# An f32r router with row transposes, weight columns by VectorE, outputs copied by ScalarE and added by transfer, statistics among the first taps

## The reference

```
x = x + attn(layernorm(x))      # Q,K,V = x@wq.T, x@wk.T, x@wv.T ; energy = K.T@V ; Q@energy*sqrt(3/64)@wo.T
x = x + ffn(layernorm(x))
# ffn, with h the normed rows (T x 256):
scores = sigmoid(h @ Wr)                      # 8 experts
_, idx = top_k(scores + router_bias, 2)
w  = scores[idx] / (sum(scores[idx]) + 1e-9)  # scattered into cw (T x 8)
hid = silu(h @ Wg[e]) * (h @ Wu[e])           # 4 MLP experts, 128 wide
routed = sum_e cw[:, e] * (hid @ Wd[e])
routed += cw[:, 4]*h + cw[:, 6]*h + cw[:, 7]*relu(h)
ffn = routed + depthwise causal conv of h over 4 rows + conv_b
```

## Time and profile before

| what | value |
|---|---|
| median of 3 runs | 886.65 us (884.33 to 886.78) |
| the profiled execution, its own time | 888.19 us |
| its span | 886.4 us |
| PE busy | 852.9 us, 96% |
| DVE busy | 751.2 us, 85% |
| ACT busy | 643.2 us, 73% |
| POOL busy | 409.6 us, 46% |
| mean granted clock of TensorE | 0.988 |

### The profile page before, as it was taken

One profiled execution on the slowest core, in us unless ns is written; L12 is line 12 of the kernel. 1 busy time (PEld: TensorE's weight loads), 2 busy tenths in 40 slices (PEclk: granted clock), 3 DMA queues, 4 the chain that ended last, 5 costly groups with the idle time before them and its releaser, 6 DMA issues.

```text
span 886.4 us, 16852 instructions
## 1 busy us (share of the span) xinstructions
PE 852.9 (96%) x5437; PEld 757.1 (85%) x5437; DVE 751.2 (85%) x2093; ACT 643.2 (73%) x1366; POOL 409.6 (46%) x585
## 2 busy tenths in 40 slices
PE   5878999999999999999999999999999999899997
PEld 4667888999889988889899998889988998788886
DVE  4668889988899988999899998999889988678884
ACT  4585867787777777787678777777867875666653
POOL 3214635554455454455355544545535544433332
PEclk9899999999999999999999999999999999999999
DMA  9112354433354442434443344554424344324434
GB/s 286 60 43 54 119 144 138 112 110 100 116 143 143 143 120 67 126 125 138 143 121 104 100 132 120 143 144 126 111 75 131 109 121 119 96 54 118 118 94 119
DMA packets 79447, 103.86 MB, mean 117 GB/s; under 512 B 6528, under 2 KB 58880, under 8 KB 79360
## 3 DMA queue, kind: packets, MB, share of 16 engines
q1 hardware_dynamic: 74752, 86.02, 30.6%
q0 software_dynamic: 4608, 16.78, 10.0%
HBM read 68.96 MB, written 17.04 MB: 97 GB/s over the span
## 4 chain that ended last, share of the span: by engine, by line
PE 77%; DVE 12%; ACT 4%; issue 3%; POOL 2%; DMA 1%; POOLq 0%; DVEq 0%; ACTq 0%
PE ps_gu L410 11%; PE ps_gu L412 10%; PE ps_gu L411 10%; PE ps_sh L541 6%; PE ps_y L410 6%; PE ps_y L411 6%; PE ps_y L412 6%; PE ps_y L460 3%; PE ps_sh L531 3%; PE ps_sh L484 2%; ACT x L842 2%; PE ps_sh L588 1%; PE ps_sh L589 1%; PE ps_gram L618 1%; PE ps_gu L564 1%
## 5 line engine op out<-in xcount | busy, mean ns | idle before, releaser
L1391 POOL TENSOR_TENSOR gate<-gate,cwb 128x512 f32<-128x512 f32 x128 | 168.0, 1313 | 291.4 <-ACT gate L765 265.6
L410 PE MATMUL ps_gu<-x2T_hi,wgu_hi 128*128 128x512 f32 x512 | 211.3, 413 | 1.2 <-DVE hid L1055 1.2
L412 PE MATMUL ps_gu<-x2T_hi,wgu_lo 128*128 128x512 f32 x512 | 202.2, 395 | 0.0
L411 PE MATMUL ps_gu<-x2T_lo,wgu_hi 128*128 128x512 f32 x512 | 201.7, 394 | 0.0
L410 PE MATMUL ps_y<-wd_hi,hid_hi 128*128 128x256 f32 x512 | 153.1, 299 | 2.2 <-DVE hid_lo L1062 2.2
L1073 DVE SCALAR_TENSOR_TENSOR conv<-x2T,conv_w,conv 128x512 f32<-128x512 f32 x192 | 150.6, 822 | 0.0
L411 PE MATMUL ps_y<-wd_lo,hid_hi 128*128 128x256 f32 x512 | 145.4, 284 | 0.0
L412 PE MATMUL ps_y<-wd_hi,hid_lo 128*128 128x256 f32 x512 | 145.0, 283 | 0.0
L1062 DVE TENSOR_TENSOR hid_lo<-hid,hid_hi 128x512 fp32r<-128x512 f32 x101 | 86.2, 853 | 46.2 <-ACT hid_hi L758 46.2
L412 PEld LDWEIGHTS ps_gu<-x2T_hi,wgu_lo 128*128 128x128 f32 x512 | 96.6, 189 | 22.2
L410 PEld LDWEIGHTS ps_gu<-x2T_hi,wgu_hi 128*128 128x128 f32 x512 | 97.2, 190 | 18.4 <-issue 2.3
(11 more groups left out here) (126 smaller groups left out, 1877.5 us busy)
## 6 DMA issues: line engine op xcount, KB each, us to landing
cwb<-cw_rows SPq DMA_DIRECT2D x128, 256.0 KB, 4.0
xa<-in_x SPq DMA_DIRECT2D x32, 512.0 KB, 7.8
acc<-in_x SPq DMA_DIRECT2D x32, 512.0 KB, 6.9
acc<-x POOLq DMA_DIRECT2D x32, 512.0 KB, 4.6
out<-acc SPq DMA_DIRECT2D x64, 256.0 KB, 2.6
cwb<-in_wg SPq DMA_DIRECT2D x4, 128.0 KB, 3.9
cwb<-in_wu SPq DMA_DIRECT2D x4, 128.0 KB, 3.7
cwb<-in_wd SPq DMA_DIRECT2D x1, 512.0 KB, 4.5
```

The costliest lines, as they stand in the source:

```text
L410: nc.tensor.matmul(dst, a_hi, b_hi, start=start, stop=False, skip_group_check=True)
L411: nc.tensor.matmul(dst, a_hi, b_lo, start=False, stop=False, skip_group_check=True)
L412: return nc.tensor.matmul(dst, a_lo, b_hi, start=False, stop=stop, skip_group_check=True)
L1391: g.tensor_tensor(gate[:, e % 2], gate[:, e % 2], cwb[:, q, e], ALU.mult).then_inc(gatew_ready, 1)
```

## The change

The router weights are split in halves side by side (`wr2`, 16 columns). `router` now multiplies with them as the stationary side, 512 rows at a time, in f32r: two products with `x2T_hi`, two with `x2T_lo`. The result is 16 x 512. ScalarE copies it (`logitsT`), TensorE turns it back in four transposes (`logits_rows`), and VectorE sums the halves (`logits_sum`). ScalarE makes the size from the sum, after `hid_hi` (1), where `mag` and `dip` now stand too. `cw` is transposed by VectorE in blocks of 32 x 32, so SP stores it in four pieces. In steps 8 to 33 ScalarE copies `ps_y` to `y_rows` and a transfer of GpSimd's queue adds it to `acc`; in the others VectorE adds as before. The aggregation of the first norm's statistics stands behind `x2T_lo` (0). In step 7 the taps are made ahead, in the head, and the statistics after them. In step 33 the residual and the second norm's statistics stand ahead of the routing.

```diff
@@
+    def by_transfer(self):
+        return self.on("Y") and self.on("C") and not self.drain()
@@ SP
                 sp.wait_ge(cwT_ready, st.before("R", 1, 1))
-                sp.dma_start(rows.rearrange("a e (t n) -> (a e t) n", t=TG), cwT[:, :]).then_inc(cw_stored, 16)
-                sp.wait_ge(cw_stored, st.before("R", 16, 16))
+                for j in range(P // SQ):
+                    sp.dma_start(rows[:, :, :].rearrange("a e (t n) -> (a e t) n", t=TG)[:, j * SQ:(j + 1) * SQ],
+                                 cwT[j * SQ:j * SQ + EM * TG, :]).then_inc(cw_stored, 16)
+                sp.wait_ge(cw_stored, st.before("R", 64, 64))
...
+                    if st.by_transfer():
+                        sp.wait_ge(y_added, st.before("Y", 16, 16))
@@ TensorE
             def router(st):
-                pe.wait_ge(x2T_ready, st.before("R", HC, HC))
+                b, q = ps_sh[0][0:2 * NE, :], st.slot("R", 2)
                 pe.wait_ge(x2Tlo_ready, st.before("R", HC, 1))
-                for t in range(TG):
-                    for c in range(HC):
-                        last = nc.tensor.matmul(b[:, t * NE:(t + 1) * NE],
-                                                x2T[:, q, c, PAD + t * P:PAD + (t + 1) * P], wr_sb[:, c],
-                                                start=(c == 0), stop=(c == HC - 1))
+                pe.wait_ge(x2Thi_ready, st.before("R", HC, HC))
+                for c in range(HC):
+                    nc.tensor.matmul(b, wr2[:, c], x2T_hi[:, q, c], start=(c == 0), stop=False,
+                                     skip_group_check=True)
+                for c in range(HC):
+                    if c == 1:
+                        pe.wait_ge(x2Tlo_ready, st.before("R", HC, HC))
+                    last = nc.tensor.matmul(b, wr2[:, c], x2T_lo[:, q, c], start=False, stop=(c == HC - 1),
+                                            skip_group_check=True)
+                last.then_inc(router_done, 1)
+
+            def logits_rows(st):
+                pe.wait_ge(logitsT_ready, st.before("R", 1, 1))
                 for t in range(TG):
+                    last = nc.tensor.transpose(ps_sh[0][:, t * 2 * NE:(t + 1) * 2 * NE],
+                                               logitsT[0:2 * NE, t * P:(t + 1) * P], ident[0:2 * NE, 0:2 * NE])
+                last.then_inc(rows_done, 1)
...
-            def weights_transpose(st):
...
@@ ScalarE
+            def y_copy(st, h):
...
+                if st.later("Y", 1):
+                    act.wait_ge(y_added, st.before("Y", 16))
+                copy(y_rows[:, 2 * h:2 * h + 2].rearrange("p t n -> p (t n)"), ps_y[h][:, :]).then_inc(out_ready, 1)
...
-            def logits_copy(st):
+            def logitsT_copy(st):
                 act.wait_ge(router_done, st.before("R", 1, 1))
+                copy(logitsT[:, :], ps_sh[0][0:2 * NE, :]).then_inc(logitsT_ready, 1)
...
             def score_size(st):
...
+                nc.scalar.activation(size[:, :], logits[:, :], ACT.Abs).then_inc(size_ready, 1)
+                act.wait_ge(size_ready, st.before("R", 1, 1))
...
-            def weights_copy(st):
@@ VectorE
                 v.tensor_tensor(cw[:, q].rearrange("p e t -> p t e"), raw[:, :, 0:NE],
                                 winv[:, :].unsqueeze(2).broadcast_to([P, TG, NE]), ALU.mult).then_inc(cw_ready, 1)
+                dve.wait_ge(cw_ready, st.before("R", 1, 1))
+                if st.later("R", 1):
+                    dve.wait_ge(cw_stored, st.before("R", 64))
+                v.transpose(cwT[:, :], cw[:, q].rearrange("p e t -> p (e t)")).then_inc(cwT_ready, 1)
+
+            def logits_sum(st):
+                dve.wait_ge(rows_done, st.before("R", 1, 1))
+                v.tensor_reduce(logits[:, :].rearrange("p (t e) -> p t e", t=TG),
+                                ps_sh[0][:, 0:TG * 2 * NE].rearrange("p (t h e) -> p t e h", t=TG, h=2), AXX, ALU.add)
...
+                if b_on and m_on and not st.on("A"):
+                    residual(st, 0)
+                    residual(st, 1)
+                    norm2_stats(st)
                 if r_on:
                     route_scores(st)
@@ GpSimd
+            def y_add(st):
+                k = st.slot("Y", 4)
+                pool.wait_ge(relu_added[st.slot("Y", 2)], st.uses("Y", 2, 16, 16))
+                pool.wait_ge(out_ready, st.before("Y", 2, 2))
+                g.dma_start(acc[:, k].rearrange("p t n -> p (t n)"), y_rows[:, :, :].rearrange("p t n -> p (t n)"),
+                            accum_op=ALU.add).then_inc(y_added, 16)
...
                     gate_weight(st, 1)
+                if st.by_transfer():
+                    y_add(st)
```

More of the change, by code:

```diff
@@ L208, in program @@
         skip_bias = sb("skip_bias", [P, 2, TG])
-        cwT = sb("cwT", [EM * TG, P])
+        SQ = 32
+        assert NE * TG == SQ
+        cwT = sb("cwT", [P, SQ])
         cwb = sb("cwb", [P, 2, EM, GT])
@@ L382, in body @@
                     k = st.slot("Y", 4)
+                    if st.by_transfer():
+                        sp.wait_ge(y_added, st.before("Y", 16, 16))
                     for h in range(2):
-                        sp.wait_ge(out_ready, st.before("Y", 2, h + 1))
+                        if not st.by_transfer():
+                            sp.wait_ge(out_ready, st.before("Y", 2, h + 1))
                         sp.dma_start(out_rows[:, bass.ds(st.group("Y") * TG + 2 * h, 2), :],
@@ L508, in xn_transpose @@
                 pe.wait_ge(xn_ready, st.before("A", TG, TG))
-                if c == 1 and st.on("R"):
-                    pe.wait_ge(cwT_ready, st.before("R", 1, 1))
-                elif st.on("B"):
+                if st.on("B"):
                     pe.wait_ge(x1_ready, st.before("B", 2, 2 - c))
@@ L523, in x2_transpose @@
                     pe.wait_ge(xnTlo_ready, st.before("A", HC, c - 1))
-                elif c == 0:
+                else:
                     pe.wait_ge(x1_ready, st.before("B", 2))
-                else:
-                    pe.wait_ge(cwT_ready, st.before("R"))
                 for t in range(TG):
@@ L740, in body @@
                     gram_halves(st)
-                if drain:
-                    down(st, "C", 2)
-                if r_on:
-                    weights_transpose(st)
                 if a_on and r_on:
                     xn_transpose(st, 0)
-                if c_on and not drain:
+                if c_on:
                     down(st, "C", 2)
@@ L909, in conv_begin @@
                         .then_inc(tap_ready, 1)
-            def weights_copy(st):
-                act.wait_ge(cwT_done, st.before("R", 1, 1))
-                if st.later("R", 1):
-                    act.wait_ge(cw_stored, st.before("R", 16))
-                copy(cwT[:, :], ps_sh[1][0:EM * TG, 0:P]).then_inc(cwT_ready, 1)
             def xnT_head(n, c):
@@ L1019, in body @@
                     norm1(st)
-                if r_on:
-                    weights_copy(st)
-                if st.on("B") and st.drain():
+                if st.on("B") and not st.on("A"):
                     norm2(st)
@@ L1031, in body @@
                     xnT_high(st, 1)
-                if st.on("B") and not st.drain():
+                if st.on("B") and st.on("A"):
                     norm2(st)
@@ L1060, in hid_low @@
                 dve.wait_ge(hidhi_ready, st.before("C", EM, e + 1))
+                if e == 0 and st.on("L") and not st.later("C", 1):
+                    dve.wait_ge(stat1, st.before("L", TG, TG))
                 k = e % 2
@@ L1063, in hid_low, with conv_tap @@
                     .then_inc(hidlo_ready[k], 1)
-            def conv_tap(st, n):
+            def conv_tap(st, n, parts=range(HC)):
                 q, k = st.slot("C", 2), PAD - 1 - n
-                for c in range(HC):
+                for c in parts:
                     if n == 0:
@@ L1185, in x2T_low @@
                 dve.wait_ge(x2Thi_ready, st.before("R", HC, c + 1))
+                if c == 0 and st.on("L") and st.later("C", 1):
+                    dve.wait_ge(stat1, st.before("L", TG, TG))
                 v.tensor_tensor(x2T_lo[:, q, c], ps_sh[c][:, :], x2T_hi[:, q, c].bitcast(F32), ALU.subtract)\
@@ L1329, in body @@
                     hid_low(st, 2)
-                if b_on and not drain:
+                if b_on and st.on("A"):
                     residual(st, 0)
```

128 lines of the change are left out of this document (80 added, 48 removed).

## The result

| | before | changed | ratio, 95% interval |
|---|---|---|---|
| median | 885.49 us (4 runs, 884.17 to 886.78) | 897.64 us (4 runs, 897.43 to 897.83) | 1.0125 (1.0105 to 1.0146) |
| profiled execution | 888.19 us, span 886.4 | 897.83 us, span 896.0 | |

The change costs 12.2 us by the medians, 9.6 by the two profiled executions. I forecast 890.6, slower by 3.9. The sign and the mechanism in the ordinary steps came out, the size did not: of the two terms of the sum, the one for steps 8 to 33 was nearly right (+12.5 against +13.7), and the one for the one-off places, -8.6, was wrong.

A forecast was written before the change was run, and what follows sets the result against it. Prediction took TensorE as the bound, with a VectorE, GpSimd and ScalarE row hooked into its loop by the change; steps 8 to 33 +12.5, one-offs -8.6, sum +3.9 on 886.65: 890.6 us, own range 885 to 896, overall 867 to 898.

The forecast's parts named there:

- The lock: GpSimd's gate multiply holds VectorE's raw: 0.66 us lost per ordinary step; H is the start of the step's third hid.
- Rival A: VectorE's raw starts ahead of GpSimd's multiply and cw waits instead, 0.3 in place of 0.7; 882.7 us, chance 0.20.
- the new wait: Router's fourth product waits for x2T_lo (1), made behind tap 1; loop 24.98 us, leaving 0.12 of the 0.48 cut.
- The chain steps: Steps into and behind the attention chain: 7 x 0.60 = +4.2 into it, 6 x -0.2 = -1.2 behind.
- The entry of 1.1: Entry from step 7 into the loop, where TensorE had slack behind its stall before: +1.1 us.
- The one-off places: Step 7's taps made in the head -5.0, head +1.3, step 33 -2.6, steps 34 to 37 -2.5, last step +0.2: -8.6.
- The head: Router's rows, copy and sum ahead of attention 1's second half delay it 1.1, weight splits 0.2: +1.3 us.
- Step 33: Step 33 to 34: a 2.3 stall at down 2 and 1.7 slow clock replace a 5.1 cost: -2.6 us.
- The drain: Steps 34 to 37: the 0.31 hid_lo wait goes, against attention 1 waiting for the logit sum: -2.5 in all.
- B: Rival: VectorE is early enough for x2T_lo (1), so TensorE stays the bound; 868.4 us, chance 0.22.
- C: Rival, a second lock: GpSimd's first gate multiply holds tap 1 about 0.6 us in 25 steps; 906 us, chance 0.13.
- The costs put at nothing: ScalarE's two y copies (0.6 each) fall into its waits; the added accumulate transfer on GpSimd's queue is covered: no cost.

The follow-up runs named there:

- e2: The changed kernel with VectorE's x2T_lo of chunk 1 ahead of tap 1 instead of behind it; 908.99 us.
- e6: e1 plus, outside the drain, tap 1 cut in two on VectorE, chunk 0 ahead of x2T_lo(1) and chunk 1 behind it; 873.22 us, ratio 0.9854.
- e1: The changed kernel with ScalarE's start of the convolution moved behind the fourth silu and its rounding, except in the drain; 882.08 us, 0.9956 of the kernel before.
- b1: The kernel before, unchanged, profiled a second time; 884.89 us, span 883.1.
- e4: The kernel before with only ScalarE's mag and dip moved behind the second rounding of hid, ahead of the acc scaling; 890.62 us, ratio 1.0041.
- e8: The kernel before with only e1's move of the convolution start behind the fourth silu; 887.66 us, ratio 1.0016.
- e7: e6 plus hid_lo(2) ahead of the routing in step 33 and y half 0 copied behind gram's transposes and x2T in chain steps; 871.06 us, ratio 0.9826.
- e3: The changed kernel with the output additions back on VectorE in every step, without y copies or accumulate transfer; 896.04 us, ratio 1.0106.

## Why the prediction was wrong in size and right in sign

**The lock: right.** `raw` was to start 0.12 behind the multiply and end at H+4.57; it starts 0.13 behind and ends at H+4.59. In 20 of the steps up to 33 it lasts 0.88 us or more, most of them 1.22. The traces show each side holding the other where it started first: in e2 and e6 the tap, started first and with 0.2 to 0.3 us left to run, held the multiply up by 0.12 us (1.42 in place of 1.30), and the multiply, once in, held a VectorE instruction by up to 1.1 (e2's pair of taps, 2.45 in place of 1.38). Rival A, `raw` first, did not happen in ordinary steps of the changed kernel. It does in the chain steps, where the multiply led by 0.39 before: there `raw` now lasts 0.19 and `cw` 1.09.

**The ordinary step: right.** Forecast 25.8, measured 25.92 in all but one, which took 26.40. e1 gives the lock's share as 0.70 (forecast 0.66, with 0.17 for the tap behind it), e6 the new wait's as 0.5. One sum in the forecast doesn't come out: its terms for the router, 1.70 less 0.93, less 0.44 to 0.50, plus 0.11, give 0.38 to 0.44, and I carried 0.48; measured is 0.39. This is 0.1 us a step and not what the forecast missed by.

**The chain steps: each kind was off, the sum nearly right by luck.** I put no router wait into the steps into a chain, because the chain step's own router comes later. But such an interval begins with the router of the ordinary step ahead, which does wait, 0.34 us. So steps into a chain cost 1.05, not 0.60; those behind one, which begin with a router that does not wait, win 0.58, not 0.2. The entry of 1.1, which I had on top, no run shows. Together they were forecast at +4.1 and came to +3.8: 3.1 too little into the chains was made up by 2.3 too little gain behind them and by the entry. Steps 8 to 33 as a whole: forecast +12.5, measured +13.7.

**The one-off places: this is the term that failed.** Forecast -8.6; measured -4.0 against the first profile of before, and -0.8 against the second (the spans, 896.0 less 883.1, less 13.7 in steps 8 to 33). Four parts:
- *Slow clock counted as a gain.* In step 7 I took 1.6 us from the clock of 0.56 behind the stall, the 3.91 us of the earlier trace rows less 2.3 that I estimated at full clock, and in step 33 let slow stretches cancel. No run shows 1.6 as the price of the stall: b1 and e4, with the same stall, made the same transposes and down products at clock 1.00 in 2.37 us (75.03 to 77.40 and 75.01 to 77.38), so the term is 1.5 where the slow clock comes and nothing where it doesn't. The stall alone does not bring this clock: of four profiles with it, two (the first of before, e8) have 0.56 behind it and two (b1, e4) have 1.00. The eight profiles without that stall of 2.9 us have no slow clock at this place, so the change may remove it where it would have come; I counted it whole, from one profile. Against b1, step 7 to 8 gained 3.0 us and not 5.0.
- *The head.* Forecast +1.3, measured +3.1 up to step 7's router: TensorE waits 1.80 for `q_lo` (0.38 before), and the gate-up products and transposes ahead of that router ran at clock 0.54, 1.4 us more. Over the eight profiles with the changed head, the time between the first router and step 7's is 23.1 to 24.1 us; over the four with the old head it is 20.84 to 20.86. So 2.2 us of this delay are there in every execution.
- *Step 33: a lock that I did not look for.* The reordered routing meets GpSimd's multiply at another instruction, and the stall behind it, before `down` 2, grows:

```profile
774.57 1.18 DVE L1170 SCALAR_TENSOR_TENSOR signed<-logits,minor 128x32 f32<-128x32 f32 x1
```

```profile
774.38 1.31 POOL L1449 TENSOR_TENSOR gate<-gate,cwb 128x512 f32<-128x512 f32 x1 [5.87 <-ACT gate L777]
```

```profile
779.39 0.38 PE L428 MATMUL ps_y<-wd_hi,hid_hi 128*128 128x256 f32 x1 [3.22 <-DVE hid_lo L1078]
```

  The stall is 3.22 us, not 2.3. With e1's move, `signed` takes 0.20 and the stall is 2.30, the forecast's figure:

```profile
764.12 0.58 PE L428 MATMUL ps_y<-wd_hi,hid_hi 128*128 128x256 f32 x1 [2.30 <-DVE hid_lo L1080]
```

  The sum was off here too: its terms, 2.3 and 1.7 in place of 5.1, give -1.1, and -1.6 with the whole cut of 0.48, where I wrote -2.6; measured is -1.7 against the first profile, +0.6 against b1. And the 1.7 for slow clock behind the new stall cost nothing: with it (e1, clock 0.50 from 763.92 to 767.33) this interval took 26.84, without it (e6) 26.82, because TensorE waits 1.49 for GpSimd's `hid_lo` there in e6.
- *The drain.* I let the wait for `hid_lo` go with `cwT`'s copy, which stood ahead of the norm on ScalarE. It grew, from 0.31 to 0.58 and more. In the rows of step 34, ScalarE's norm starts at 804.91 though GpSimd's factors are done at 803.36:

```profile
804.91 2.08 ACT L865 ACTIVATE x<-acc,shift,rstd 128x256 f32<-128x256 f32 x4 [2.59 <-issue]
```

```profile
800.29 0.93 POOL L1462 DMA_DIRECT2D acc<-x  x1 [3.94 <-ACT x L1024]
803.16 0.20 POOL L1433 TENSOR_TENSOR shift<-negm,rstd 128x4 f32<-128x4 f32 x1
```

  What is left in the code is the relu transfer, which must have read `x2` before the norm overwrites it; it lands 4.5 us after its issue (804.84), and in steps 34 to 36 the norm starts 0.07 us behind that landing each time. In step 35, where the transfer takes 5.2 us, the interval is 22.92 in place of 22.3. Its start moved from H+0.98 to H+1.29, because ScalarE scales and makes the relu behind the moved `size`, `mag` and `dip`. This is read from rows and code; no run tried it. GpSimd's first multiply of the next step also waits longer for `cwb`, from H+10.9 to H+11.8; that the four small stores do it is likely and not shown. In all, steps 34 to 37 came 0.25 us longer, where I had them 2.5 shorter. The last step made up for part of it: 1.2 shorter, where I had it 0.2 longer.

Unrounded, the misses against the first profile sum to 5.7 us: 2.4 up to step 8, 1.2 in steps 8 to 33, 0.9 at step 33, 1.3 behind it. The other 2.5 of the measured 12.2 is that the profiled execution of before was 2.7 us above the median; I took it as 1.5 above, and subtracted from it what other executions don't have.

**Rivals.** B (the loop doesn't close, 868.4) is what e6 and e7 make true by two and four moves, at 873.2 and 871.1. A occurred in chain steps and, in e2, in ordinary ones. C did not occur in the changed kernel and did in e2. The costs put at nothing held in the ordinary steps of e3, and the copy ahead of gram's, counted at 0.4 a step, cost 0.3.

## What to carry to other kernels

A cheaper product on the bounding engine pays nothing while the change hooks a second row of work into its loop: follow that row from a fixed point of the step, and ask which of its instructions run beside one that holds them up, as the multiply held `raw` by 1.03 us (1.22 in place of 0.19). Here the multiply started ahead of `raw` with and without the loss. What cost 0.7 us a step was that its lead shrank from 0.83 to 0.13 us, so that `raw` waited for nearly all of it; moving 1.5 us of work that nobody waits for behind the silu gave that back. Price one-off places by more than one profile of the kernel before: what stands in one of them only can't be counted whole.

## What the runs showed that I had not expected

- A stall of 2.91 us is followed by 3.9 us at clock 0.56 in one execution (and in e8's), and one of 2.92 us at the same place by clock 1.00 in another (and in e4's); with the place at step 33 this is 3.8 of 885 us. The 19 runs of the kernel before beside e1 to e4 lay between 883.45 and 890.84; how much of that is this clock isn't shown.
- The same lock costs 0.12 us or 1.1 us, by who comes first and how much of it is left: a VectorE tap near its end holds GpSimd's multiply for 0.12, and the multiply, just started, holds a 0.19 us instruction for nearly all of its own 1.3. `MATCH_REPLACE8` rows keep their 0.14 us beside a running multiply (e1, 498.15 to 498.72), and `hid` keeps its 0.68 (e6, at 479.84, the multiply running from 479.65).
- A 32x32-block transpose of `cw` on VectorE takes 0.21 us, and `hid_lo` starts 0.38 behind `cw` where it started 0.10 behind it (0.28; estimated at 0.25).
